# Attention and mixture-of-experts layer on one core: the maxima's row by single DMAs, projections as row tiles, and a new order on four queues

## The reference

```python
xn = _layernorm(x, axis=-1)
s = _L0_attn_ref(xn, w_down_q, w_down_kv, w_up_q, w_up_k, w_up_v, w_out, ln_scale, ln_bias)
g = _silu(_L0_ffn_ref(xn, router_w, w1, w2))       # 8 experts, the best 2 of each token, capacity 2561
return x + s * g

# attention: 16 heads of 64
h = layernorm(xn) * ln_scale + ln_bias
c_q, c_kv = h @ w_down_q.T, h @ w_down_kv.T        # 128 wide
q, k, v = c_q @ w_up_q.T, c_kv @ w_up_k.T, c_kv @ w_up_v.T
q, k = rope(q), rope(k)
attn = softmax(q k' / 8)
out = (attn v) @ w_out.T + xn
```

## Time and profile before

| | us |
|---|---|
| three runs | 3657.8, 3653.6, 3657.75 |
| median | 3657.75 |
| profiled execution | 3655.32 |
| its span | 3653.8 |
| TensorE busy | 3599.4 (99%) |
| VectorE busy | 3195.1 (87%) |
| ScalarE busy | 2759.1 (76%) |
| GpSimd busy | 1199.8 (33%) |

### The profile page before, as it was taken

How to read it: one execution, slowest core, us unless ns; L and a number is a source line. 1 busy time by engine, 2 the same in 40 slices (tenths; PEclk the granted TensorE clock), 3 DMA queues, 4 the chain that set the end, 5 groups by cost and what they waited for, 6 DMA issues and landing times. The chain is left out here.

```text
span 3653.8 us, 77190 instructions
## 1 busy us (share of the span) xinstructions
PE 3599.4 (99%) x24217; PEld 2364.0 (65%) x24217; DVE 3195.1 (87%) x4341; ACT 2759.1 (76%) x4016; POOL 1199.8 (33%) x1178
## 2 busy tenths in 40 slices
PE   7999999999999999999999999999999999999999
PEld 5754554545544554545554555454699999999999
DVE  8889999999999999999999999999777777777799
ACT  5778888888878888888888888888766666666665
POOL 2212222222222222222222222232366666666400
PEclk9999999999999999999999999999999999999999
DMA  7985767676666666666667676765666666666798
GB/s 257 358 283 142 185 156 186 157 185 161 180 160 176 170 174 169 171 171 166 177 165 181 160 186 156 184 162 136 193 222 215 217 223 216 214 224 216 235 369 274
DMA packets 378436, 724.74 MB, mean 198 GB/s; under 512 B 105277, under 2 KB 253886, under 8 KB 342272
## 3 DMA queue, kind: packets, MB, share of 16 engines
q0 software_dynamic: 83504, 340.66, 36.2%
q1 hardware_dynamic: 294864, 383.23, 31.8%
HBM read 453.60 MB, written 138.81 MB: 162 GB/s over the span
## 5 line engine op out<-in xcount | busy, mean ns | idle before, releaser
L1180 ACT ACTIVATE at_ex<-at_st 128x1024 f32<-128x1024 f32 x1024 | 1048.8, 1025 | 138.3 <-PE at_st L1327 132.8
L1383 PE MATMUL at_pv<-at_ex,at_v 128*64 128x512 f32 x4096 | 991.6, 605 | 0.0
L1037 DVE TENSOR_REDUCE at_mx<-at_fr 128x1 fp32r<-128x512 f32 x1024 | 705.9, 689 | 202.5 <-PE at_fr L1393 169.6
L1204 ACT ACTIVATE at_fr<-at_fr 128x512 f32<-128x512 f32 x1024 | 603.4, 589 | 243.0 <-PE at_fr L1393 229.7
L1383 PEld LDWEIGHTS at_pv<-at_ex,at_v 128*64 128x64 f32 x4096 | 248.3, 136 | 471.1 <-issue 462.2
L1050 DVE TENSOR_TENSOR at_sum<-at_sum,at_ex 128x1024 f32<-128x1024 f32 x448 | 545.3, 1217 | 3.7 <-ACT at_ex L1180 3.4
L1393 PE MATMUL at_fr<-at_kfar,at_qh 64*128 64x512 f32 x1024 | 459.7, 449 | 5.9 <-DVE at_mx L1037 4.5
L1390 PE MATMUL at_fr<-at_kdif,at_qh 64*128 64x512 f32 x1024 | 461.4, 451 | 1.8 <-DVE at_mx L1037 0.9
L1327 PE MATMUL at_st<-at_qh,at_kh 64*128 64x512 f32 x2048 | 452.8, 392 | 3.8 <-DMA at_top<-at_mneg 3.7
L1390 PEld LDWEIGHTS at_fr<-at_kdif,at_qh 64*128 64x128 f32 x1024 | 187.7, 183 | 413.7 <-issue 356.9
L1327 PE MATMUL at_st<-at_ql,at_kh 64*128 64x512 f32 x2048 | 452.0, 391 | 0.0
(11 more groups left out here) (213 smaller groups left out, 6359.4 us busy)
## 6 DMA issues: line engine op xcount, KB each, us to landing
at_cq<-scr_c SPq DMA_DIRECT2D x62, 1024.0 KB, 6.1
at_ck<-scr_c SPq DMA_DIRECT2D x62, 1024.0 KB, 5.2
at_sum<-at_sum POOLq DMA_DIRECT2D x95, 512.0 KB, 6.0
scr_v<-pj_v SPq DMA_DIRECT2D x64, 512.0 KB, 6.8
at_v<-scr_v SPq DMA_DIRECT2D x64, 512.0 KB, 6.6
mid_rec<-scr_rec SPq DMA_DIRECT2D x256, 128.0 KB, 5.1
scr_o<-mid_oT SPq DMA_DIRECT2D x64, 512.0 KB, 3.0
at_rotq<-at_swpq POOLq DMA_DIRECT2D x126, 256.0 KB, 4.6
```

Of the source, the lines that this page charges most:

```text
L1037: e.reduce_max(mx[k // QB][:, h * QB + k % QB:h * QB + k % QB + 1], fr[h][:, :], AX.X).then_inc(s_tr[h], 1)
L1180: e.activation(ex[k][:, :, :], st[u % 2][:, :, :], ACT.Exp, scale=SCALE).then_inc(s_exp, 1)
L1204: e.activation(fr[h][:, :], fr[h][:, :], ACT.Relu).then_inc(s_pos[h], 1)
L1383: mm = e.matmul(pv[n][rows[h], :], v[i.u][:, kt, rows[h]], ex[kt][:, h, :], start=(kt == 0), stop=(kt == KT - 1))
```

## The change

**Rows of maxima.** turn_maxima, negate and mneg are gone. one_row holds -1.0 instead of 1.0, so that the fourth pass subtracts by itself. SyncE copies each column of mx, 128 partitions of one 4-byte element, into its 128 places of the row of top as soon as VectorE has made it: max_row, 16 DMAs a pair instead of four.

**Projections.** The first half of each projection is made as row tiles too: the keys' in turn 2, the queries' in turn 6. scores_free, upper_rows and lower_rows are otherwise as before; the second half's row tiles wait until the first half's copy has emptied the bank. side_ready is gone.

**SyncE.** The broadcasts of the reciprocals (each) move from the end of the body into turns 0 to 2 of the next one; store comes ahead of gather as before.

**ScalarE.** The four copies of the projections are in turns 2, 3, 6 and 7; high(one, K) moves from the end of turn 2 into turn 3; out_copy(prev, 1) stands behind the first rectifier of turn 1; far_keys is made a turn 7 earlier, for pair i+2 instead of i+1 in turn 1.

**VectorE.** low(one, Q) moves from turn 1 to turn 2; the keys' products are turn_cos at the end of turn 4 and turn_sin at the head of turn 5, instead of cos at the head and sin at the end of turn 5.

The diff, cut to the parts spoken of:

```diff
@@ -848,12 +846,12 @@
                 wait_apart(e, s_pv, j.n(UNITS, -UNITS), s_apart_s)
                 e.dma_start(v[j.u][:, :, :], scr["v"].rearrange("b p t (r m) -> b r p t m", r=HP)[j.n() // HP, j.n() % HP, :, :, :]).then_inc(s_ldv[j.u], 16)
-            def max_rows(j, n):
-                e.wait_ge(s_neg, j.n(2, n + 1))
-                for h in range(2):
-                    r = rows[h].start
-                    e.dma_start(top[j.u][r:r + 1, bank[n]].bitcast(F32).rearrange("o (t q) -> o t q", q=P),
-                                mneg[n][h * QB:(h + 1) * QB, :].bitcast(F32)).then_inc(s_mrow[n], 16)
+            def max_row(j, k, h):
+                wait_apart(e, s_tr[h], j.n(NSLOT_Q, k + 1), s_apart_s)
+                r, col = rows[h].start, h * QB + k % QB
+                e.dma_start(top[j.u][r:r + 1, k * P:(k + 1) * P].bitcast(F32), mx[k // QB][:, col:col + 1].bitcast(F32),
+                            allow_slow_non_contiguous=True).then_inc(s_mrow[k // QB], 16)
             def spread(i, halves, k=0):
                 e.wait_ge(s_de, i.n(1, k + 1))
@@ -862,10 +860,18 @@
                         r = 32 * (2 * h + n)
                         e.dma_start(denc[:, h, n, :], den[k][r:r + 1, :].rearrange("o (p k) -> o p k", p=P)).then_inc(s_denc, 16)
-            def broadcast(i, halves, k=0):
+            def gather(i, halves, k=0):
                 e.wait_ge(s_recc, i.n(1, k + 1))
                 for n in halves:
                     e.dma_start(scr["rec"][i.n(), n:4:2, :].rearrange("h (p k) -> p h k", p=P), recc[:, :, n, :]).then_inc(s_recd, 16)
+            def each(i, n):
+                e.wait_ge(s_recd, i.n(32, 32))
+                for h in range(2):
...
@@ -897,27 +904,51 @@
                 if ahead == 1:
                     e.wait_ge(s_scat, 32 * NPAIR)
                     ex_sync["slots"](e)
+                one = i.next(1)
+                older = prev and not (isinstance(i.n(), int) and i.n() < 2)
                 if ahead >= 3:
                     load(i.next(3), Q)
+                max_row(i, 5, 1)
+                max_row(i, 6, 0)
+                if older:
+                    each(prev.next(-1), 0)
+                max_row(i, 6, 1)
+                max_row(i, 7, 0)
+                max_row(i, 7, 1)
+                if older:
+                    each(prev.next(-1), 1)
                 if ahead:
-                    load_v(i.next(1))
-                max_rows(i, 1)
+                    load_v(one)
+                    max_row(one, 0, 0)
+                    max_row(one, 0, 1)
+                    max_row(one, 1, 0)
                 if ahead >= 3:
                     load(i.next(3), K)
+                if ahead:
+                    max_row(one, 1, 1)
+                    max_row(one, 2, 0)
                 if prev:
                     spread(prev, (0, 1))
                 if ahead:
-                    max_rows(i.next(1), 0)
+                    max_row(one, 2, 1)
+                    for k in (3, 4):
+                        for h in range(2):
+                            max_row(one, k, h)
+                    max_row(one, 5, 0)
                 if prev:
-                    if not (isinstance(i.n(), int) and i.n() < 2):
+                    if older:
                         store(prev.next(-1))
-                    broadcast(prev, (0, 1))
+                    gather(prev, (0, 1))
...
@@ -1032,7 +1063,7 @@
             def maximum(j, k, h, ready):
                 if k % QB == 0 and h == 0:
-                    wait(e, s_tf, j.n(2, k // QB - 1))
+                    wait(e, s_mrow[k // QB], j.n(32 * QB))
                 e.wait_ge(ready, j.n(NSLOT_Q, k + 2 - (h == 0)))
                 e.reduce_max(mx[k // QB][:, h * QB + k % QB:h * QB + k % QB + 1], fr[h][:, :], AX.X).then_inc(s_tr[h], 1)
@@ -1120,7 +1150,7 @@
                     if g == 3 and most:
                         turn_cos(two, Q)
                     if g == 5 and most:
-                        turn_cos(two, K)
+                        turn_sin(two, K)
                     if g == 7 and more:
                         low(one, K)
                     early, late = additions(i, prev, g)
@@ -1130,14 +1160,14 @@
                         maximum(*slot_of(i, g), 0, s_y)
                     for added in late:
                         add_keys(*added)
-                    if g == 1 and more:
+                    if g == 2 and more:
                         low(one, Q)
                     if g == 3 and most:
                         turn_sin(two, Q)
                     if g == 4 and older:
                         normalise(prev.next(-1), 0)
-                    if g == 5 and most:
-                        turn_sin(two, K)
+                    if g == 4 and most:
+                        turn_cos(two, K)
                     if g == 7 and prev:
                         recip(prev)
                     if g == 7 and older:
@@ -1273,30 +1295,30 @@
                         out_copy(i, 0)
                     if g < 2 or more:
                         gain(*slot_of(i, g), 0, s_x)
-                    if g == 0 and prev and ahead >= 2:
-                        proj_copy(two, Q, 1, pv[0])
-                    if g == 4 and ahead >= 2:
-                        proj_copy(two, K, 1, pv[1])
+                    if g == 1 and prev:
+                        out_copy(prev, 1)
+                    if g == 3 and more:
+                        high(one, K)
                     exps(i, 2 * g)
                     if g < 2 or more:
                         gain(*slot_of(i, g), 1, s_y)
+                    if g == 2 and ahead >= 2:
+                        proj_copy(two, K, 0, pv[1])
+                    if g == 6 and ahead >= 3:
+                        proj_copy(three, Q, 0, pv[0])
+                    if g == 7 and ahead >= 2:
+                        far_keys(two)
                     exps(i, 2 * g + 1)
                     if g == 4 and prev:
                         den_copy(prev, 1)
-                    if g == 1 and ahead >= 2:
-                        proj_copy(two, K, 0, pv[1])
-                    if g == 2:
-                        negate(i, 1)
-                    if g == 5 and ahead >= 3:
-                        proj_copy(three, Q, 0, pv[0])
-                    if g == 6 and more:
-                        negate(one, 0)
+                    if g == 3 and ahead >= 2:
+                        proj_copy(two, K, 1, pv[1])
+                    if g == 7 and ahead >= 3:
+                        proj_copy(three, Q, 1, pv[0])
                     if g == 0 and more:
                         high(one, Q)
...
                 if u % KT == 0:
-                    e.wait_ge(s_mrow[u // KT], i.n(32, 32))
+                    e.wait_ge(s_mrow[u // KT], i.n(32 * QB, 32 * QB))
                 wait(e, s_exp, i.n(UNITS, u - 1))
...
-            def upper_rows(i, u, j, x, dst):
+            def upper_rows(i, u, j, x, n, dst):
+                if n == 0:
+                    e.wait_ge(s_ld[x][j.u], j.same(32, 32))
                 scores_free(i, u)
                 for k in range(3):
-                    mm = project_row(j, x, k, 0, dst)
+                    mm = project_row(j, x, n, k, 0, dst)
                     if k == 2:
                         mm.then_inc(s_upper, 1)
                     score(i, u, k, 1)
@@ -1361,14 +1385,14 @@
                         mm.then_inc(s_st, 1)
                     score(i, u + 1, k, 1)
-            def lower_rows(i, u, j, x, dst):
-                e.wait_ge(s_upper, i.n(2, 1 if x == K else 2))
+            def lower_rows(i, u, j, x, n, dst):
+                e.wait_ge(s_upper, i.n(4, n + (1 if x == K else 3)))
                 for k in range(3):
                     mm = score(i, u + 1, k, 0)
                     if k == 2:
                         mm.then_inc(s_st, 1)
-                    mm = project_row(j, x, k, 1, dst)
+                    mm = project_row(j, x, n, k, 1, dst)
                 mm.then_inc(s_pr, 1)
             def values(i, u, emptied, behind=True):
@@ -1519,43 +1535,32 @@
                 def split(g):
-                    if g == 3 and ahead >= 2:
-                        e.wait_ge(s_neg, i.n(2, 2))
-                        return two, K, pv[1]
-                    if g == 7 and ahead >= 3:
-                        e.wait_ge(s_neg, one.n(2, 1))
-                        return three, Q, pv[0]
-                def side_ready(g):
-                    if g == 1 and ahead >= 2:
+                    if g == 2 and ahead >= 2:
                         if prev:
                             e.wait_ge(s_osb, i.n(2, 0))
                         else:
                             e.wait_ge(s_raw[Q], 6)
+                        return two, K, 0, pv[1]
+                    if g == 3 and ahead >= 2:
+                        e.wait_ge(s_raw[K], two.n(2, 1))
+                        return two, K, 1, pv[1]
+                    if g == 6 and ahead >= 3:
+                        e.wait_ge(s_osb, i.n(2, 1))
```

(30 more changed lines are left out.)

49 lines of the change are left out of this document (18 added, 31 removed).

## The result

The changed kernel took a median of 3598.97 us (3598.51 to 3601.02, 4 runs), the kernel before 3657.78 us (3653.6 to 3658.27, 4 runs): a ratio of 0.9843, 95% interval 0.9826 to 0.986. Forecast: 3604. The profiled execution took 3598.52 us, its span 3597.0 against 3653.8.

The account below looks back on a forecast made before the run. TensorE, busy all the time without waits, was taken as the bound: 61 pairs x 0.84 = 51.2 us, with the last pairs and prologue 52.4, off the median of 3657.75 gives 3605.3, off the profiled run 3602.9: 3604, range 3594 to 3634.

Parts of the forecast that it names:

- TensorE's sum: TensorE, all turns: 2.20 us a pair taken out, 1.36 added, so 0.84 less a pair; 52.4 us in all.
- The 1.01 in turn 1: TensorE, turn 1: cost of the whole projection there, 4.93 less the base of 3.92.
- Forecast cover 0.9: ScalarE: first-half copy ends about 1519.05, TensorE wants its bank at 1519.96; cover 0.9 us, less a signal.
- where I said 0.3: Rival: ScalarE's copies 1.2 us late, turns 3 and 7 each wait 0.3, 37 us given back, 3641; chance 0.07.
- The budget by turns: VectorE: work of 3.5 to 5.2 us a turn set against TensorE's turns of 3.92 to 5.40.
- the sentence on the lag: VectorE, level turns 2 and 3: maxima stand at a turn's head, so half a microsecond of lag reaches nobody.
- Cost nothing: VectorE: no work added, 33.8 us needed of 36.04 a pair, so no loss expected.
- The bounds of 0 and 2.03: SyncE, 16 column issues a pair: 0 at one end, 16 x 2.03 = 32.5 us at the other.
- SyncE becomes the bound: Rival: columns occupy queue or ring over 1.39 us each, scores wait; at 2.03, +575, about 4230 us; chance 0.08.
- The broadcasts' move: SyncE: broadcasts moved into the next pair's turns 0 to 2, wanted in turns 4 and 7; cost nothing.
- The 8.3 us: SyncE: time left from a half's last maximum for its column's issue, landing and two broadcasts ahead of it.
- the far keys' copy: ScalarE, turn 7: copy 11.9 us from turn 5's start, sum landed 8.5, worst 11.6; rival of lateness 3647 to 3659, chance 0.05.

Follow-up runs that it names:

- e1: Kernel before with only the 16 column DMAs in place of transposes and negations, and SyncE's new order; projections, ScalarE and VectorE orders as before: 3632.57 us.
- e5: Changed kernel with the queries' first half projected whole at the end of turn 5, not as row tiles in turn 6: 3613.39 us.
- e6: Changed kernel with the keys' first half projected whole at the end of turn 1, not as row tiles in turn 2: 3638.83 us.
- e4: Changed kernel with the copy of each projection's first half behind the last exponential of turns 2 and 6 on ScalarE, not ahead of it: 3628.26 us.
- e2: Changed kernel with VectorE's order of before: both keys' products in turn 5, the queries' low part in turn 1: 3650.81 us.
- e7: Changed kernel with each column of maxima sent twice, the copy meeting zero weights, 32 column DMAs a pair: 3747.61 us.
- e3: Changed kernel with the reciprocals' four broadcasts back at the end of SyncE's body: 3633.84 us.
- e8: Changed kernel with each column of maxima sent three times, the copies meeting zero weights, 48 column DMAs a pair: 4322.63 us.

## Why the prediction was right, point by point

**TensorE's sum.** Right. Every turn came within 0.04 us of its forecast, the pair at 36.01 against 36.04. e1 and e5 take the sum apart: the transposes were worth 0.33 (forecast 0.30), a whole half 0.21 more than its row tiles (0.89 - 0.68). The 1.01 in turn 1 was read as the projection's; e6 puts 0.88 there, and the other 0.13 went with the old surroundings.

**The 5 us below.** The span fell 56.8, the sum was 52.4. The difference lies in single pairs. By the heads of its turns, seven of 61 turns 4 of the kernel before are longer than the usual 5.39, by 0.1 to 0.8 us and 3.4 in all. The view of waits puts four of them, 1.7 us, down to the row of maxima. In the changed kernel no turn 4 is more than 0.12 off the usual 5.36. One of the seven in TensorE's timeline of the kernel before, and the waits of the kernel before and the changed one from 2400 to 2700 us:

```profile
1039.81 0.50 PE L1327 MATMUL at_st<-at_qh,at_kh 64*128 64x512 f32 x2 [0.58 <-DMA at_top<-at_mneg]
```

```profile
PE at_st L1327 <- DMA at_top<-at_mneg: 2.0, 1, 2.0
```

```profile
PE at_st L1349 <- DMA at_top<-at_mx: 0.4, 1, 0.4
```

The seven turns and the last pair's wait make 5.0 us of the 57.4 between the first and the last denominators, and 52.4 are left for the sum. The sum was right, then, and a term was missing: I took the pair of the earlier trace rows to stand for all of them. The average of 36.86 does not prove that, since a shorter pair at the end (34.5 us) makes up for the long ones. In e1 the waits of the loop are gone too, and one of 1.7 us near the end is left.

**ScalarE.** Right. Forecast cover 0.9, measured 0.84; e4 shows what its loss costs, 0.24 to 0.27 a turn where I said 0.3.

**VectorE.** The budget by turns was right, the sentence on the lag was wrong. That "a lag there of half a microsecond reaches nobody" is what e2 and e6 refute: in e2 0.62 of lag cost 0.42 in turn 2, and turn 6 lost 0.48. The cover is about a third of a microsecond, since step_y waits for the maximum of step_x. That 3604 was right all the same rests on the level turns 2 and 3 having no lag at all, which by the prediction's own reasoning was luck: the head of turn 3 in the changed kernel's VectorE timeline is

```profile
1522.20 0.69 DVE L1068 TENSOR_REDUCE at_mx<-at_fr 128x1 fp32r<-128x512 f32 x1
```

0.55 into the turn, right behind step_x's end. "Cost nothing" therefore hung on a cover that I had not reckoned, and the move that I called a way to keep turn 5 inside carries, with that of the low part, 52 us.

**SyncE.** Occupied 26.1, forecast 24 to 30; a column 0.67 to 0.77, taken 0.6 to 1.0. The bounds of 0 and 2.03 were far out on both sides. That SyncE becomes the bound once a column takes more than its room was right: e7 crosses that point, with half the room for each, and is slower by 2.5% than the kernel before.

**The broadcasts' move.** "Nothing" was right for the place that they have, and hid what the move is for: e3 loses 35 us without it. The 8.3 us that I counted for the last column from its maximum on are 7.8 from its issue on in the changed kernel, and 4.1 in e3, where arrivals of up to 6.2 us no longer fit.

**GpSimd.** Right: the keys' sums are issued 3.1 us into turn 5, forecast 3.0, and the far keys' copy starts at 1543.62, 11.96 in, forecast 11.9. The landings, line 969 against the earlier trace rows's 3.7/4.7/7.8, came 0.9 later at the median and no later at the worst; the worst, 7.7 behind an issue that ends 4.0 in, is 0.3 ahead of that copy:

```profile
DMA to landing us min/median/max: 4.8/5.6/7.7
```

## What to carry to other kernels

Where TensorE is full, price an edit by slots in its timeline, turn by turn; it comes out to hundredths. Then ask of each engine beside it not for its idle time per pair but whether its queue fits each turn, and how far into the turn the first result is wanted: here an engine idle for 7% of the time could cost 52 us by order alone. Small DMAs off the path are cheap until issue time times count fills the queue. Ask also how long before its use the last of them is issued: waits of the issuing engine and bulk transfers ahead of it eat this lead, in some pairs and not in others.

## What the runs showed of the hardware

A DMA of one 4-byte element from each of 128 partitions is issued in 0.52 us at the median, less than the 0.60 of the spread with its runs of 16 bytes, and takes 0.67 to 0.77 us of SyncE all told. Single ones take about 2 us (1.986 in the changed kernel, 2.251 in e8). Behind four broadcasts and a 1024 KB load in the same queue the last of five such columns took 6.1 us to arrive, behind the broadcasts alone, in the last pair of e3, 8.2; where the trace of e8 tells it, the median is 3.0. And work freed on an engine is not the same as freed time: in e6 TensorE had 0.69 us less to do in turn 2, and its next turn took 0.42 longer.
